# Four reorderings inside one attention round of a two-block macaron model on one Trainium2 core

## The chip, the cores and the metric

The program runs on one core of one Trainium2 chip. The metric is the device time of one execution in microseconds; lower is better. The engines are TensorE (PE in the profile; its weight loads are PEld), VectorE (DVE), ScalarE (ACT), GpSimd (POOL) and SyncE (SP, which here only issues DMAs). Each engine works through its own instruction queue in the order in which the program lists it, and the engines meet only at semaphores.

## The reference, cut to what matters

The input x has 16 sequences of 256 tokens and 128 channels, all in f32. Six residual blocks follow one another:

```
x = x + 0.5 * L0_ffn(layernorm(x))     # gated feed-forward with token shift
x = x + L0_attn(layernorm(x))          # causal attention, 16 heads of 8
x = x + 0.5 * L0_ffn(layernorm(x))     # the same feed-forward again
x = x + 0.5 * L1_ffn(layernorm(x))     # mixture of 8 experts, top 2
x = x + L1_attn(layernorm(x))          # "focus": attention iterated up to 3 times
x = x + 0.5 * L1_ffn(layernorm(x))     # the mixture again
```

The change touches the first three of them. The feed-forward (the gated one) mixes each token with the one before it, `xr = mu_r*x + (1-mu_r)*x_prev` and `xk` likewise, and gives `sigmoid(xr @ W_r) * (relu(xk @ W_k)**2 @ W_v)`. The causal attention clips its scores, takes a softmax with small epsilons in both denominators, multiplies with the values and projects the result.

## The kernel before, in words

The first three blocks run as one software pipeline over the 16 sequences, from about 55 us to 400 us of the trace. One round n (`causal_round` in each engine's program) does the attention of sequence n and, between its pieces, parts of other sequences: the normalisation and the projection behind the attention of n-1, the second feed-forward of n-2, the normalised tokens, queries, keys and values of n+2, the first feed-forward of n+3, and the statistics and normalised tokens of n+4. Rounds 0 and 1 are written out, rounds 2 to 11 are a loop of two rounds per turn, and rounds 12 to 15 are written out again. `within(n, low, high)` says which parts a written-out round has; `first` is the first feed-forward (rounds 0 to 12), `second` the second one (from round 2), `before` the back of the attention of n-1 (from round 1), `ahead` the front of n+2 (to round 13).

A round has eight steps, one for each pair of heads, hp = 0 to 7. For every pair TensorE computes the scores twice: queries in rows (`row_scores`, L1632 to L1635, into `ps_q`), of which VectorE takes the maxima (`row_maxima`, L2497, `mx`), and keys in rows (`causal_scores`, L1645 and L1646, into `ps_k`), which ScalarE exponentiates (`causal_exps`, L1173, into `e_buf`). GpSimd zeroes the part above the diagonal (L829, "keep"). For every four heads TensorE then multiplies with the values (`causal_values`, L1661 and L1658, into `ps_o`), and ScalarE copies the sums out (`evacuate_group`, L1049, `o_sb<-ps_o`).

The queues are orders written out by hand, and these waits matter for the change:

- Layer norms. VectorE takes mean and variance (`front_norm`, L2434 and L2438). ScalarE makes 1/std from them in two instructions (`token_norm`, L1054 `lnv<-mv` and L1056 `rstd<-lnv`). VectorE applies them (`front_normed`, L2443, `y<-x,mv,rstd`), and `ln_apply` waits for that `rstd`. The statistics of norm1(n+4) are applied at the very end of VectorE's round n, behind the last two maxima, `all_maxima` (L2503 to L2505) and the gating of the second feed-forward (L2466); the next instruction on VectorE is the first maximum of round n+1. The norm of n-2 behind the attention has buffers of its own (`lnv_k`, `rstd_k`, `mv_k`, `y_b`).
- Back of the attention of n-1. TensorE turns the sums over to tokens in two halves (`causal_back`, L1558, `ps_m<-ident,o_sb`) through one bank. Its second half waits for `fast_o_read`, which VectorE raises when `causal_sums(b, 0)` (L2516 and L2517) has read the first half. VectorE normalises (`causal_normalise`, L2535 to L2541, giving `o_tok`), TensorE transposes (`causal_out`, L1558, `ps_m<-ident,o_tok`), ScalarE copies (`causal_out`, L1049, `o_t`), and TensorE projects (`causal_project`, L1688).
- First feed-forward of n+3. GpSimd makes the token difference (L765), VectorE the two mixed inputs (`mix_inputs`, L2459 `xr` and L2460 `xk`, both shown as `mix<-mix,cols,y_t`), TensorE the hidden products (`ffn_hidden`, L1572 and L1574), ScalarE five activations on them (`ffn_hidden`, L1073 to L1080), GpSimd the square and gate (L769, L774), TensorE the output (L1580), ScalarE the sigmoid (L1084), VectorE the gating (L2466), and GpSimd the residual add (L779, `x<-x,mix`).
- Scores. `row_scores` of a pair waits for the maxima of the pair before it in the same bank, and `causal_scores` for the exponentials of the pair before it, since both banks are used again at once.
- `squared_lengths` (L1621) follows the last value product of the round before on TensorE, and `longest` (L2487, `qk_max`) reads it on VectorE between the maxima of pairs 0 and 1.
- `value_sums` (L1697 to L1701) ends TensorE's round; ScalarE copies it (`vs<-ps_m`).

## Time and profile before

| | |
|---|---|
| median of 3 runs | 1514.51 us (1509.53 to 1516.96) |
| the profiled execution | 1516.96 us, span 1515.2 us |
| mean granted TensorE clock | 0.962 of full speed |
| busy over the span | PE 90%, DVE 67%, ACT 57%, POOL 33% |
| causal rounds, pair 0 of round 0 to the last maximum | 55.1 to 398 us |

The span is the time from the first instruction to the last; the execution adds 1.8 us around it. The busy share of an engine is an average over stages: in the looped rounds VectorE is at 89%, not 67%. Durations are those of one profiled execution, and a duration of an instruction that overlaps the next one is longer than the distance between their starts. In a timeline row the number in square brackets is the engine's idle time in front of the instruction, with the instruction that ended it; gaps of about 0.1 us are not shown.

### The profile page before, as it was taken

Reading aid. Unit: us, or ns where it says so; the run is one execution under the profiler, and the core shown is the slowest. Engines: PE = TensorE matmul, PEld = TensorE weight load, DVE = VectorE, ACT = ScalarE, POOL = GpSimd, SP = SyncE. Lnnn points to the kernel's source line nnn. Section 1 sums busy time; section 2 is a strip of 40 time slices with the busy share of each in tenths; the row PEclk is TensorE's granted clock in tenths of the full one; section 3 lists DMA queues with packets and bytes.
Section 4 is the critical chain, followed back from the end, with each engine's and each line's share of the span. In section 5 each row is a group of like instructions: output and inputs, shape, how many; then the busy total and the mean of one; then the engine's idle time right before and its main releaser. Section 6 shows DMA issues by size and latency. Waiting matters only on the chain. (4 is left out here: it accounts for less than half of the span.)

```text
span 1515.2 us, 37569 instructions
## 1 busy us (share of the span) xinstructions
PE 1357.4 (90%) x11749; PEld 938.8 (62%) x11749; DVE 1009.2 (67%) x3281; ACT 871.2 (57%) x1595; POOL 499.1 (33%) x786
## 2 busy tenths in 40 slices
PE   4798999998689999999889998989899999899998
PEld 2566666666457777777455555555555555566876
DVE  3689889887636767677565565666666666577544
ACT  3577777776333434344567776777656667333453
POOL 5366656664210000012233233323222222004444
PEclk9799999999779999999899998999989999899999
DMA  5332233223030000001444544454534444001232
GB/s 147 76 85 64 62 83 83 57 71 83 1 86 1 12 11 11 11 11 48 120 114 125 138 121 100 124 130 111 128 93 109 112 114 102 3 8 50 83 117 77
DMA packets 75213, 116.69 MB, mean 77 GB/s; under 512 B 9401, under 2 KB 60753, under 8 KB 65876
## 3 DMA queue, kind: packets, MB, share of 16 engines
q1 hardware_dynamic: 73044, 111.05, 28.7%
q0 software_dynamic: 2048, 4.20, 0.9%
q8 instruction: 56, 0.92, 0.2%
q14 instruction: 65, 0.53, 0.1%
HBM read 85.72 MB, written 29.37 MB: 76 GB/s over the span
## 5 line engine op out<-in xcount | busy, mean ns | idle before, releaser
L1356 ACT ACTIVATE e_buf<-ps_q 128x1024 f32<-128x1024 f32 x192 | 196.5, 1023 | 106.3 <-PE ps_q L2068 106.1
L2079 PE MATMUL ps_o<-e_buf,v_st 128*32 128x256 f32 x3072 | 212.6, 396 | 4.3 <-POOL v_st L938 3.9
L1356 ACT ACTIVATE e_buf<-ps_k 128x1024 f32<-128x1024 f32 x192 | 195.6, 1019 | 19.4 <-PE ps_k L2068 17.5
L1931 PEld LDWEIGHTS ps_o<-w,e_buf 128*128 128x128 f32 x1536 | 182.8, 193 | 15.3 <-issue 13.9
L1931 PE MATMUL ps_o<-w,e_buf 128*128 128x128 f32 x1536 | 190.3, 278 | 0.0
L3023 DVE COPY o_sb<-ps_o 128x256 f32<-128x256 f32 x192 | 80.9, 422 | 113.0 <-PE ps_o L2079 68.4
L2497 DVE TENSOR_REDUCE mx<-ps_q 128x3 f32<-128x384 f32 x256 | 130.3, 548 | 27.7 <-PE ps_q L1635 27.0
L2068 PE MATMUL ps_q<-q_st,k_st 73*128 73x256 bf16 x768 | 120.6, 281 | 18.3 <-DMA q_st<-scr_q 17.6
L1173 ACT ACTIVATE e_buf<-ps_k 128x768 f32<-128x768 f32 x128 | 103.3, 807 | 48.1 <-PE ps_k L1646 46.0
L2079 PEld LDWEIGHTS ps_o<-e_buf,v_st 128*32 128x32 f32 x3072 | 81.8, 111 | 76.8 <-issue 34.5
L2068 PEld LDWEIGHTS ps_q<-q_st,k_st 73*128 73x128 bf16 x768 | 60.7, 99 | 105.5 <-issue 70.2
L1272 ACT ACTIVATE e_buf<-ps_q,b_t 128x512 f32<-128x512 f32 x96 | 65.5, 685 | 99.3 <-PE ps_q L1923 96.6
L2068 PE MATMUL ps_k<-q_st,k_st 73*128 73x256 bf16 x768 | 119.4, 279 | 3.2 <-ACT e_buf L1356 1.1
L1272 ACT ACTIVATE e_buf<-ps_k,b_t 128x512 f32<-128x512 f32 x96 | 64.8, 686 | 95.7 <-PE ps_k L1923 93.8
L829 POOL TENSOR_SCALAR_AFFINE_SELECT e_buf<-e_buf 128x512 f32<-128x512 f32 x128 | 85.7, 669 | 92.6 <-ACT e_buf L1173 91.1
L1558 PE MATMUL ps_m<-ident,o_sb 128*128 128x128 f32 x508 | 79.5, 280 | 10.5 <-DVE o_tok L2517 2.9
L1923 PE MATMUL ps_q<-mix,w 128*128 128x512 f32 x176 | 85.1, 607 | 2.5 <-issue 2.5
L2068 PEld LDWEIGHTS ps_k<-q_st,k_st 73*128 73x128 bf16 x768 | 72.9, 100 | 22.1 <-ACT e_buf L1356 13.5
L1923 PE MATMUL ps_k<-mix,w 128*128 128x512 f32 x176 | 85.1, 607 | 0.0
L912 POOL TENSOR_TENSOR rest<-qk,parts 128x512 f32<-128x512 f32 x6 | 6.9, 1156 | 235.7 <-ACT parts L1049 235.7
L1632 PE MATMUL ps_q<-mask_q,ident_b 128*128 128x256 bf16 x256 | 72.9, 285 | 9.3 <-DVEq L3311 4.5
L2774 DVE SCALAR_TENSOR_TENSOR e_buf<-ps_o,lexp,e_buf 128x128 f32<-128x128 f32 x192 | 54.0, 344 | 36.4 <-PE ps_o L1931 33.2
(397 smaller groups left out, 2913.5 us busy)
## 6 DMA issues: line engine op xcount, KB each, us to landing
q_st<-scr_q SPq DMA_DIRECT2D x64, 576.0 KB
k_st<-scr_k SPq DMA_DIRECT2D x192, 192.0 KB
scr_q<-parts SPq DMA_DIRECT2D x64, 192.0 KB, 2.1
scr_k<-parts SPq DMA_DIRECT2D x84, 64.0 KB
slots_in<-heads_out SPq DMA_DIRECT2D x2, 1536.0 KB
slots_out<-heads_out SPq DMA_DIRECT2D x12, 256.0 KB, 2.1
heads_out<-slots_in SPq DMA_DIRECT2D x10, 256.0 KB, 3.3
out_dram<-x SPq DMA_DIRECT2D x8, 256.0 KB
```

Source lines behind the costliest of these rows:

```text
L829: pool.affine_select(out=e, in_=e, compare_op=ALU.is_ge, fill=0.0, base=0, pattern=[[0, 2], [0, 2], [1, P]], channel_multiplier=-1)\
L1173: act.activation(e_buf[g % 2][:, hp * 2 % HG:hp * 2 % HG + 2, 0:3 * P], ps_k[:, :, 0:3 * P], ACT.Exp, bias=SHIFT).then_inc(sem("fast_exp"), 1)
L1272: act.activation(h_sb[e % 2][:, f, :], bank, ACT.Relu, bias=b1_t[:, j:j + 1])\
L1356: act.activation(e_buf[g % 2][:, hp * 2 % HG:hp * 2 % HG + 2, :], (ps_q, ps_k)[hp % 2][:, :, :], ACT.Exp).then_inc(sem("fast_exp"), 1)
L1558: return pe.transpose(dst, src, ident[0:k, 0:k])
L1632: mm(o[:, P:3 * P], ident_b[:, :], mask_q[:, :], start=True, stop=False, skip_group_check=True)
L1923: mm(bank, w1[:, e, f * P:(f + 1) * P], mixed(m, u)[:, :], start=True, stop=True)\
L1931: last = mm(ps_o[:, e % 2, t * P:(t + 1) * P], h_sb[e % 2][:, f, t * P:(t + 1) * P], w2[:, e * NF + f, :], start=f == 0, stop=f == NF - 1)
L2068: last = mm(bank[:, u, t * T:(t + 1) * T], k_st[p][0:ROWS_P1, hp * 2 + u, t * P:(t + 1) * P], q_st[p][0:ROWS_P1, hp * 2 + u, :], start=Tru ...
L2079: last = mm(ps_o[VW * j:VW * j + VW, g % 2, 0:T], v_st[p][:, kt, HG * g + j, :], e_buf[g % 2][:, j, kt * T:(kt + 1) * T], start=kt == 0, s ...
L2497: red(mx[:, h, :], ps_q[:, u, 0:3 * P].rearrange("p (c k) -> p c k", c=3), AX.X, ALU.max)\
L3023: dve.tensor_copy(o_sb[:, g, :], ps_o[:, g % 2, 0:T]).then_inc(sem("fast_evac"), 1)
```

## The change

Four places of the round change their order; nothing is added or taken away.

```diff
--- before.py
+++ after.py
@@ -1215,9 +1215,9 @@
                 causal_exps(n, 4)
                 if isinstance(n, int) and n == B - 2:
                     mix_norm(0)
-                evacuate_group(n, 1)
                 if before:
                     causal_out(n - 1)
+                evacuate_group(n, 1)
                 causal_exps(n, 5)
                 if ahead:
                     normed_tokens(n + 2)
@@ -1233,12 +1233,12 @@
                 evacuate_group(n, 2)
                 if second:
                     ffn_sigmoid(mix2(n - 2))
-                if within(n, 0, B - 5):
-                    token_norm(norm1(n + 4), mv, lnv, rstd)
                 causal_exps(n, 7)
                 if ahead:
                     causal_values(n + 2)
                 value_sums(n)
+                if within(n, 0, B - 5):
+                    token_norm(norm1(n + 4), mv, lnv, rstd)
                 if before:
                     token_norm(norm3(n - 1), mv_k, lnv_k, rstd_k)
 
@@ -1735,9 +1735,9 @@
                         if first:
                             ffn_out(mix1(n + 3), 0)
                     elif hp == 4:
-                        causal_values(n, p, 1)
                         if before:
                             causal_out(b)
+                        causal_values(n, p, 1)
                     elif hp == 5:
                         if before:
                             causal_project(b)
@@ -2586,10 +2586,10 @@
                 if within(n, B - 2, B - 2) and isinstance(n, int):
                     dve.wait_ge(sem("F_x"), mix2(GB - 1) + 1 + 1)
                     mix_stats(0, 0)
+                if first:
+                    mix_inputs(mix1(n + 3))
                 if before:
                     causal_sums(b, 0)
-                if first:
-                    mix_inputs(mix1(n + 3))
                 row_maxima(n, 2)
                 if before:
                     causal_sums(b, 1)
```

1. ScalarE copies the transposed attention output of n-1 (`causal_out`) ahead of the second group of sums (`evacuate_group(n, 1)`).
2. ScalarE makes 1/std for norm1(n+4) (`token_norm`) behind the last exponentials, the copy of the values and the copy of the value sums, where it stood ahead of all three.
3. TensorE transposes the attention output of n-1 ahead of the second value product.
4. VectorE makes the mixed inputs of the first feed-forward ahead of the first half of the attention sums.

ScalarE's queue at the end of the second round (n = 1), the difference of the two programs; `lnv` and `rstd` are the norm that is moved, `v_tok` and `vs` the two copies, `lnv_k` and `rstd_k` the norm behind the attention:

```order
 L1159 ACTIVATE squares<-qk 128x512
 L1049 ACTIVATE o_sb<-ps_o 128x256
-L1054 ACTIVATE lnv<-mv 128x2
-L1056 ACTIVATE rstd<-lnv 128x2
 L1173 ACTIVATE e_buf<-ps_k 128x2x384
 L1049 ACTIVATE v_tok<-ps_m 128x256
 L1049 ACTIVATE vs<-ps_m 128x384
+L1054 ACTIVATE lnv<-mv 128x2
+L1056 ACTIVATE rstd<-lnv 128x2
 L1054 ACTIVATE lnv_k<-mv_k 128x2
 L1056 ACTIVATE rstd_k<-lnv_k 128x2
```

The two instructions of the norm pass the exponentials of pair 7 and both copies, and now stand directly ahead of the other norm. SyncE's and GpSimd's queues stay as they are.

VectorE's queue in an early round, from `longest` to the sums; `mix<-mix,cols,y_t` are xr and xk, `s_sum` and `o_tok` the first half of the attention sums:

```order
 L2487 TENSOR_REDUCE qk_max<-ps_o 16x2
 L2497 TENSOR_REDUCE mx<-ps_q 128x3 x2
+L2459 SCALAR_TENSOR_TENSOR mix<-mix,cols,y_t 128x256
+L2460 SCALAR_TENSOR_TENSOR mix<-mix,cols,y_t 128x256
 L2516 TENSOR_SCALAR s_sum<-ps_m,low_behind 128x16
 L2517 SCALAR_TENSOR_TENSOR o_tok<-vs,ps_m 128x128
-L2459 SCALAR_TENSOR_TENSOR mix<-mix,cols,y_t 128x256
-L2460 SCALAR_TENSOR_TENSOR mix<-mix,cols,y_t 128x256
 L2497 TENSOR_REDUCE mx<-ps_q 128x3 x2
 L2516 TENSOR_SCALAR s_sum<-ps_m,low_behind 128x16
```

Four instructions change places in pairs: the mixed inputs now come first, and the read of the first half, which frees the bank, second.

TensorE's queue at pair 4 of an early round; `ps_o<-e_buf,v_st` is the second value product, `ps_m<-ident,o_tok` the transposes of the attention output:

```order
 L1645 MATMUL ps_k<-q_st,k_st 128x128
 L1646 MATMUL ps_k<-q_st,k_st 128x256
-L1661 MATMUL ps_o<-e_buf,v_st 32x256 x4
-L1658 MATMUL ps_o<-e_buf,v_st 32x128 x4
 L1558 MATMUL ps_m<-ident,o_tok 128x128 x2
+L1661 MATMUL ps_o<-e_buf,v_st 32x256 x4
+L1658 MATMUL ps_o<-e_buf,v_st 32x128 x4
 L1632 MATMUL ps_q<-mask_q,ident_b 128x256
 L1633 MATMUL ps_q<-k_st,q_st 128x256
```

The two transposes pass the eight small products of the value group.

## Rows read from the trace of the kernel before

**Rows 1.** Windows: ten looped rounds, then a stretch of the last rounds.
```profile
core 0: us, PE busy (x) PEld busy (x) DVE busy (x) ACT busy (x) POOL busy (x), PEclk, DMA share, GB/s
93.90:311.80 217.90, 198.78 (x2032) 149.04 (x2030) 193.22 (x561) 162.74 (x410) 139.21 (x199) 1.00 0.29 73
...
364.70:371.50 6.80, 6.19 (x32) 5.15 (x33) 4.21 (x11) 2.45 (x6) 1.25 (x2) 0.50 0.54 122
```

**Rows 2.** Timeline of VectorE around one looped round (the eighth), from its start.
```profile
start us, us, engine line op out<-in xcount [idle before <-releaser]
...
202.28 0.59 DVE L2443 TENSOR_SCALAR y<-x,mv,rstd 128x128 f32 x2
202.80 1.01 DVE L2497 TENSOR_REDUCE mx<-ps_q 128x3 f32<-128x384 f32 x2
203.88 0.92 DVE L2443 TENSOR_SCALAR y<-x,mv_k,rstd_k 128x128 f32 x2
205.18 0.68 DVE L2487 TENSOR_REDUCE qk_max<-ps_o 16x512 f32 x1 [0.38 <-PE ps_o L1621]
205.79 1.00 DVE L2497 TENSOR_REDUCE mx<-ps_q 128x3 f32<-128x384 f32 x2
...
207.14 0.79 DVE L2459 SCALAR_TENSOR_TENSOR mix<-mix,cols,y_t 128x256 f32<-128x256 f32 x1
207.85 0.85 DVE L2460 SCALAR_TENSOR_TENSOR mix<-mix,cols,y_t 128x256 f32<-128x256 f32 x1
...
215.96 0.47 DVE L2460 SCALAR_TENSOR_TENSOR mix<-mix,cols,y_t 128x256 f32<-128x256 f32 x1
...
216.69 0.59 DVE L2443 TENSOR_SCALAR y<-x,mv,rstd 128x128 f32 x2
...
222.16 1.02 DVE L2497 TENSOR_REDUCE mx<-ps_q 128x3 f32<-128x384 f32 x2 [1.04 <-PE ps_q L1635]
...
224.13 0.59 DVE L2443 TENSOR_SCALAR y<-x,mv,rstd 128x128 f32 x2
```

**Rows 3.** Timeline of ScalarE, same round: its start and its last third.
```profile
201.74 0.19 ACT L1054 ACTIVATE lnv<-mv 128x2 f32<-128x2 f32 x1
201.97 0.20 ACT L1056 ACTIVATE rstd<-lnv 128x2 f32<-128x2 f32 x1
202.08 0.79 ACT L1173 ACTIVATE e_buf<-ps_k 128x768 f32<-128x768 f32 x1
...
203.03 0.49 ACT L1049 ACTIVATE vs<-ps_m 128x384 f32<-128x384 f32 x1
203.40 0.21 ACT L1054 ACTIVATE lnv_k<-mv_k 128x2 f32<-128x2 f32 x1
...
218.69 0.38 ACT L1073 ACTIVATE mix<-ps_o 128x256 f32<-128x256 f32 x1 [0.50 <-PE ps_o L1574]
...
223.81 0.20 ACT L1056 ACTIVATE rstd<-lnv 128x2 f32<-128x2 f32 x1
```

**Rows 4.** Timeline of GpSimd, same round: the residual add.
```profile
203.73 0.73 POOL L779 TENSOR_TENSOR x<-x,mix 128x256 f32 x1
```

**Rows 5.** Timeline of TensorE, same round.
```profile
206.48 0.27 PE L1632 MATMUL ps_q<-mask_q,ident_b 128*128 128x256 bf16 x1
...
207.46 0.60 PE L1558 MATMUL ps_m<-ident,o_sb 128*128 128x128 f32 x4
208.76 0.71 PE L1572 MATMUL ps_m<-w_t,mix 128*128 128x128 f32 x4 [0.69 <-DVE mix L2460]
...
213.81 0.64 PE L1661 MATMUL ps_o<-e_buf,v_st 128*32 128x256 f32 x8
...
214.77 0.44 PE L1558 MATMUL ps_m<-ident,o_tok 128*128 128x128 f32 x2
215.24 0.28 PE L1632 MATMUL ps_q<-mask_q,ident_b 128*128 128x256 bf16 x1
...
217.33 0.44 PE L1558 MATMUL ps_m<-ident,y 128*128 128x128 f32 x2 [0.41 <-DVE y L2443]
```

**Rows 6.** Waits in the ten looped rounds: VectorE on the squared lengths.
```profile
DVE qk_max L2487 <- PE ps_o L1621: 3.5, 9, 0.4
```

**Rows 7.** Timeline of VectorE at the start of the second round.
```profile
74.32 1.02 DVE L2497 TENSOR_REDUCE mx<-ps_q 128x3 f32<-128x384 f32 x2 [0.39 <-issue]
```

**Rows 8.** Timeline of TensorE in the fifteenth round.
```profile
365.31 0.40 PE L1632 MATMUL ps_q<-mask_q,ident_b 128*128 128x256 bf16 x1 [1.47 <-DVE mx L2497]
```

## The prediction

> **What bounds the kernel now.** I read the windows by stage first, since all four edits lie in the causal rounds. The ten looped rounds take 217.9 us, 21.79 us each, with VectorE busy for 193.22 us (89%) and TensorE for 198.78 us (91%) at a granted clock of 1.00 [rows 1]. The reader is to see that no engine is full, but two are near it, so a round is a ring through several queues. Its length is found by following one thing round, and I follow the normalised tokens `y` of norm1(n+4), the last instruction of VectorE's round.
>
> They start at 202.28, and again at 224.13, 21.85 us later [rows 2]. From 202.28 VectorE works through its queue to the other `y` (norm2), which ends at 216.69 + 0.59 = 217.28. In these 15.00 us the one idle time worth naming is 0.38 us before `longest`, ended by the squared lengths on TensorE [rows 2]. TensorE has waited 0.41 us for that `y` and starts on it at 217.33 [rows 5]; ScalarE gets the products at 218.69 after 0.50 us of idle time, and from there to the `rstd` of norm1 at 223.81 its queue has eleven rows and no wait for another engine [rows 3]. That `rstd` ends at 224.01, and `y` starts 0.12 us later [rows 2, 3]. One round earlier it is the same: end 201.97 + 0.20 = 202.17, `y` at 202.28. So the ring is 15.00 us of VectorE and 6.85 us of TensorE and ScalarE, and `rstd` stands on it with no slack. The 1.04 us that VectorE idles before the maxima of pair 7 at 222.16 [rows 2] is a wait inside the second part and not spare time behind it.
>
> **The norm on ScalarE (edit 2).** It removes nothing and moves two instructions behind three. Now the exponentials of pair 7 start at 202.08, `lnv` at 201.74. After the edit the exponentials take the place of `lnv` (201.74, 0.34 us earlier), `vs` follows 203.03 - 202.08 = 0.95 us behind them at 202.69, the next instruction 203.40 - 203.03 = 0.37 us later at 203.06, and `rstd` 0.23 us after that, ending at 203.49 [rows 3]. That is 1.32 us later than 202.17. VectorE's `y` would start at 203.60 instead of 202.28. Behind it on VectorE stand the maxima of pair 0, for which TensorE waits before pair 1, and everything else of the round. The norm of n-2 keeps its time (its `lnv_k` now starts at 203.40 as before, since the same work is ahead of it).
>
> Of the 1.32 us the idle time before `longest` gives 0.38 us back, as VectorE then arrives after the squared lengths; it is up to 0.4 us and 3.5 us in nine of the loop's rounds [rows 6]. Nothing else in the 15.00 us is idle, so the maxima of pair 1 come at 205.79 + 0.94 = 206.73. The second part of the ring grows by the whole 1.32 us. The ring is longer by 0.94 us. This holds for the ten looped rounds: 9.4 us. Rounds 0 and 1 have the same end of round, but the first maximum behind round 0 idles 0.39 us anyway [rows 7], and both lose the wait at `longest`: 1.32 - 0.39 - 0.38, about 0.6 us, twice, 1.2 us. Rounds 12 to 15 have no norm1. Sum: 10.6 us.
>
> **What collides.** The times of VectorE depend on GpSimd beside it. The `y` of norm n-2 took 0.92 us, the other `y` of the same shape 0.59 [rows 2], while GpSimd's residual add ran from 203.73 to 204.46 [rows 4]. After the edit the add comes 0.34 us earlier (it follows the last "keep", which follows the exponentials), to 203.39 to 204.12, and it then lies under the moved `y` at 203.60. I take the 0.33 us as moved from one `y` to the other, cost 0. The ends are a gain of 0.33 us a round, if nothing collides, and a loss of 0.5 us; over 12 rounds -4 to +6 us.
> The Trainium skill ("SBUF — State Buffer", section "Who interferes with whom") says that VectorE in a two-port mode and GpSimd take a shared port pair by an exclusive lock, and that the second to issue blocks fully. The row bears it out: the tail of the slowed `y` is 204.80 = 204.46 + 0.34. By that rule the moved `y` would stand until 204.12, 0.52 us, where the old one lost 0.33, and the sum would be about 2 us higher.
>
> **The mixed inputs on VectorE (edit 4).** Now the first half of the sums is read from 206.79 (205.79 + 1.00), the mixed inputs run 207.14 to 208.70, and TensorE, 0.69 us idle, starts the hidden products at 208.76 [rows 2, 5]. The inputs would come 0.35 us earlier. But TensorE's second half of the transposes stands ahead of the hidden products, and it needs the bank that the first half's read frees. It starts at 207.46 without a wait now; after the edit it can start only when inputs and read are both done, at 208.70 plus the shift of the round, and the hidden products 0.44 us behind it. So the edit gains nothing and makes the hidden products about 0.4 us later. I cost it at nothing for the ring; what hides it is VectorE's own work between the read of the sums and the maxima of pair 3 (the second half of the sums, the denominators, the statistics of norm2). If that cover were gone it would cost 0.4 us in each of 13 rounds, 5 us.
>
> **The transposes on TensorE and the copy on ScalarE (edits 3 and 1).** The transposes start at 214.77, as soon as `o_tok` is there, so the value group now fills the time ahead of them [rows 5]. It goes from 213.81 to about 214.6. After the edit it runs behind them: transposes to 215.05 (0.28 us), value group to 215.85, and so the scores of pair 5 start 0.6 us later than 215.24, where the second of them waited for VectorE's maxima anyway. The 0.41 us of idle time at 217.33 and that wait cover it, barely [rows 5]. Cost 0, ends -0.1 (the projection comes sooner) and +0.3 us a round.
>
> **The clock.** With both halves late, TensorE would wait twice within a short stretch: before pair 2, which it starts at 206.48 now and which then needs the first of the two maxima from 206.73, there at 207.23, 0.75 us; and before the second transposes, where it arrives about 0.8 us later than the 207.46 of now and VectorE is done at 208.70 + 0.94 = 209.64, 1.4 us. Nothing like it stands in the looped rounds of before, whose clock never left 1.00 [rows 1]. In the fifteenth round TensorE waited 1.47 us in one piece [rows 8], and the 6.8 us from 364.7 on ran at 0.50, that is at 1.2 GHz instead of 2.4 [rows 1]. Two microseconds of waiting so close together may do the same. The 6.8 us at half the clock cost TensorE at most 3.4 us of work. Its waits and VectorE's own chain cover much of that, so I take five such falls in the ten rounds at 0.8 us each, a quarter of it: 4 us. The ends are none (0) and one in each round at half of it, 1.7 us (17).
>
> **The sum.** 10.6 + 0 + 0 + 0 + 4 = 14.6 us. Against the profiled execution (1516.96 us: span 1515.2 and 1.8 around it) that gives 1531.6. It was the slowest of the three; its median is 2.45 us lower, and against the median I forecast 1529.
>
> **The rivals.**
> - Faster. The exponentials and the "keep" of pair 7 come 0.34 us earlier, so the last value group and the squared lengths come earlier, and the 0.38 us before `longest` vanish without a price. That decides if `rstd` has 0.94 us or more of slack before `y`; then 12 rounds give 12 x 0.38 = 4.6 us, and with half a microsecond a round from the earlier inputs up to 10: 1505 to 1510. For it: the wait at `longest` is real [rows 6]. Against it: 0.12 us between `rstd` and `y`, in both rounds shown. Chance 0.05.
> - The shift is swallowed. The collisions with GpSimd dissolve (0.33 us in `y`, and something of the 0.79 and 0.85 us of the mixed inputs, where the same two instructions take 0.47 for the second feed-forward [rows 2]), as VectorE slips against it; with 0.6 us of that gained it is 0.94 - 0.6 = 0.34 us a round and no clock falls: 4 us, 1518.5. For it: GpSimd's chain hangs on ScalarE and does not slip along at first. Against it: its cast and third split simply follow under the same two instructions. Chance 0.11.
> - The edits stay beside the path, because the ring is elsewhere: 1514.5. Against it stands that the ring closes to 0.1 us. Chance 0.03.
> - The clock falls in every looped round: 10.6 + 17 = 28 us, 1542. For it: two waits of 2.1 us in sum. Against it: rounds and clock need not keep step. Chance 0.06.
> - My forecast, 8 to 24 us slower: 0.75.
>
> **How the numbers follow.** A difference within 0.5% (7.6 us) is about what measurement can't tell from none. Slower by more: 0.75 + 0.06 and a little of the second rival, 0.82. The same: 0.13. Faster: 0.05. The range takes 10.6 us with the collisions' gain (-4) at the lower end, 1521, widened to 1520 for the second rival, and at the upper end 10.6 + 4 + 6 + half of what more the clock may take, 1541.
>
> **What would show it.** In the profile after, `rstd` of norm1 stands between `vs` and `lnv_k`, and VectorE idles about 1.2 us before the last `y` of rounds 0 to 11. The idle time at `longest` is gone. TensorE idles over 1 us before the second `ps_m<-ident,o_sb` group, and its 0.69 us before L1572 are gone. A looped round lasts 22.7 us, or 23.5 with a fall of the clock, and stretches at 0.50 appear between 94 and 320 us. A looped round at or below 21.8 us, or a `y` that starts as early against the maxima of pair 7 as now, would prove the main step wrong; a clock of 1.00 throughout, the last term.

## The result, and the profile after

| | before | after |
|---|---|---|
| median of 4 runs | 1512.28 us (1509.53 to 1516.96) | 1533.62 us (1530.47 to 1540.83) |
| the profiled execution | 1516.96 us, span 1515.2 | 1536.57 us, span 1534.8 |
| mean granted TensorE clock | 0.962 | 0.955 |

The ratio is 1.0156, with a 95% interval of 1.0126 to 1.0187: slower by 21.3 us by the medians and by 19.6 us by the two profiled executions. The forecast was 14.6 us slower than the profiled execution, 1529 us at the median, with a range of 1520 to 1541. The direction held and the result lies in the range; the size was too small, by 5.0 us of 19.6.

The windows show where it went. The columns are those of [rows 1], the first row is the ten looped rounds again, and the second is one of the short stretches in which the clock fell.

```profile
core 0: us, PE busy (x) PEld busy (x) DVE busy (x) ACT busy (x) POOL busy (x), PEclk, DMA share, GB/s
92.30:329.40 237.10, 203.85 (x2032) 153.93 (x2031) 196.31 (x560) 160.98 (x410) 140.07 (x199) 0.96 0.26 67
...
194.50:197.90 3.40, 3.40 (x18) 2.50 (x22) 2.52 (x11) 0.54 (x2) 1.30 (x3) 0.50 0.27 77
```

The rounds take 237.1 us instead of 217.9. That is 19.2 of the 19.6 us. Rounds 12 to 15 add 4.0 us, the stretch ahead of the loop is 0.4 us shorter, and everything behind round 15 is 3.2 us shorter. VectorE does only 3 us more work than in [rows 1] and TensorE 5 us more, so most of the new time is waiting. The clock is at 0.96 over the stretch, where it was at 1.00: it fell six times, at 122.8, 146.7, 194.5, 218.4, 266.1 and 290.0. The last row is the third of these falls, at 0.50, the lower level of 1.2 GHz; each of the six lasted 3.4 us. I take a round from one `top<-mx` (L2504, once a round) to the next. The ten were 21.25 to 22.38 us long before and 21.79 on average. Now the four without a fall last 22.48 to 23.04 us (the first 22.48, the others 22.85 to 23.04) and the six with one 24.15 to 24.41.

The loop has two rounds per turn, and its steady rounds (those without a fall, from n = 4 on) alternate between two kinds: before, 21.84 us for odd n and 21.74 for even n. The kinds differ inside as well: [rows 2] is an odd round (n = 7, the eighth), where `y<-x,mv_k,rstd_k` takes 0.92 us, and in the even rounds it takes 0.70.

This is VectorE in the seventh round of after (n = 6, a looped round, with a fall in it), from its start, answering [rows 2]. The idle time before an instruction and what ended it stand in brackets, as there.

```profile
188.34 0.82 DVE L2443 TENSOR_SCALAR y<-x,mv,rstd 128x128 f32 x2 [1.19 <-ACT rstd L1056]
189.08 1.02 DVE L2497 TENSOR_REDUCE mx<-ps_q 128x3 f32<-128x384 f32 x2
190.02 1.24 DVE L2443 TENSOR_SCALAR y<-x,mv_k,rstd_k 128x128 f32 x2
191.18 0.67 DVE L2487 TENSOR_REDUCE qk_max<-ps_o 16x512 f32 x1
191.78 1.00 DVE L2497 TENSOR_REDUCE mx<-ps_q 128x3 f32<-128x384 f32 x2
192.71 0.63 DVE L2459 SCALAR_TENSOR_TENSOR mix<-mix,cols,y_t 128x256 f32<-128x256 f32 x1
193.27 0.84 DVE L2460 SCALAR_TENSOR_TENSOR mix<-mix,cols,y_t 128x256 f32<-128x256 f32 x1
...
195.77 0.23 DVE L2516 TENSOR_SCALAR s_sum<-ps_m,low_behind 128x16 f32<-128x16 f32 x1 [0.39 <-PE ps_m L1558]
...
198.93 1.02 DVE L2497 TENSOR_REDUCE mx<-ps_q 128x3 f32<-128x384 f32 x2 [1.02 <-PE ps_q L1635]
```

The reader is to see four things. `y` now waits 1.19 us for `rstd`. The idle time before `qk_max` is gone. The two `y` and the mixed inputs have durations other than before (this is an even round: before, its two `y` take 0.59 and 0.70 us). And behind the fall at 194.5 there are two new waits for TensorE, 0.39 and 1.02 us.

ScalarE at the same place, answering [rows 3]: the norm behind the copies, as the order said.

```profile
186.53 0.80 ACT L1173 ACTIVATE e_buf<-ps_k 128x768 f32<-128x768 f32 x1
187.22 0.38 ACT L1049 ACTIVATE v_tok<-ps_m 128x256 f32<-128x256 f32 x1
187.48 0.50 ACT L1049 ACTIVATE vs<-ps_m 128x384 f32<-128x384 f32 x1
187.85 0.22 ACT L1054 ACTIVATE lnv<-mv 128x2 f32<-128x2 f32 x1
188.10 0.20 ACT L1056 ACTIVATE rstd<-lnv 128x2 f32<-128x2 f32 x1
```

TensorE in the same round, answering [rows 5]. The first row's wait stands before pair 2, the second's before the second half of the transposes, the third's before those of the attention output. L1572 has no wait any more.

```profile
192.38 0.28 PE L1632 MATMUL ps_q<-mask_q,ident_b 128*128 128x256 bf16 x1 [1.00 <-DVE mx L2497]
...
194.50 1.11 PE L1558 MATMUL ps_m<-ident,o_sb 128*128 128x128 f32 x4 [0.89 <-DVE o_tok L2517]
195.41 1.06 PE L1572 MATMUL ps_m<-w_t,mix 128*128 128x128 f32 x4
...
202.12 0.44 PE L1558 MATMUL ps_m<-ident,o_tok 128*128 128x128 f32 x2 [1.18 <-DVE o_tok L2541]
```

The first hidden products (L1572) take 1.06 us instead of 0.71 [rows 5], at half the clock.

### The profile page after: what moved, and what is told of

The parts are those of the page before. It is cut to its first block and busy times, and to the rows that moved or that the text cites. A ratio compares the mean times of both kernels' runs of the same rounds, so it can differ in the third digit from the quotient of the medians.

```text
span 1534.8 us, 37569 instructions
## 1 busy us (share of the span) xinstructions
PE 1361.5 (89%) x11749; PEld 946.6 (62%) x11749; DVE 1013.5 (66%) x3281; ACT 869.0 (57%) x1595; POOL 499.0 (33%) x786
## 5 line engine op out<-in xcount | busy, mean ns | idle before, releaser
L829 POOL TENSOR_SCALAR_AFFINE_SELECT e_buf<-e_buf 128x512 f32<-128x512 f32 x128 | 84.1, 657 | 96.4 <-ACT e_buf L1173 93.7
L1558 PE MATMUL ps_m<-ident,o_sb 128*128 128x128 f32 x508 | 83.2, 289 | 20.9 <-DVE o_tok L2517 13.3
L1558 PEld LDWEIGHTS ps_m<-ident,o_sb 128*128 128x128 f32 x508 | 60.0, 146 | 33.2 <-DVE o_tok L2517 16.7
```

The source lines that it names most:

```text
L829: pool.affine_select(out=e, in_=e, compare_op=ALU.is_ge, fill=0.0, base=0, pattern=[[0, 2], [0, 2], [1, P]], channel_multiplier=-1)\
L1558: return pe.transpose(dst, src, ident[0:k, 0:k])
```

## The experiments

norm_only, inputs_only, out_only and all_but_norm were timed beside runs of the kernel before that took 1570 us; beside the others it took 1514. No trace of the kernel before is kept from there. The trace of out_only shows steady rounds of 21.72 and 21.82 us, as long as those of before, and the 55 us behind the causal rounds; their cause was not examined. So only ratios to the runs of before beside them, and the lengths of the looped rounds, are compared. The expectations were written when the result of after was known; the 20 or 21 us that they name are its loss.

**norm_only: edit 2 alone.**

```diff
-                if within(n, 0, B - 5):
-                    token_norm(norm1(n + 4), mv, lnv, rstd)
                 causal_exps(n, 7)
...
                 value_sums(n)
+                if within(n, 0, B - 5):
+                    token_norm(norm1(n + 4), mv, lnv, rstd)
```

> Edit 2 alone (1/std of norm1(n+4) behind the copies on ScalarE). Ring theory: a looped round is 22.8 to 23.2 us instead of 21.8, VectorE idle about 1.2 us before the last y, which over 12 rounds is 12 to 14 us; TensorE's waits before pair 2 and before the hidden products come to 1.6 us a round and are less close together, so at most three falls of the clock at 1.3 us: 12 to 18 us slower in all. Rival (the swap on VectorE and TensorE's second wait carry most of it): under 7 us slower.

Ratio 1.0033 (1.0018 to 1.0047). The looped rounds took 223.1 us, +5.2, of which about 1.5 is one fall of the clock. The steady rounds lasted 22.07 (odd) and 22.27 (even), where before they lasted 21.84 and 21.74: +0.24 and +0.52, +0.38 us on average. The time is that of the rival (under 7 us), but its reason is not: the wait that the ring theory named is there. VectorE in an odd round:

```profile
251.69 0.91 DVE L2443 TENSOR_SCALAR y<-x,mv,rstd 128x128 f32 x2 [1.19 <-ACT rstd L1056]
...
253.45 0.95 DVE L2443 TENSOR_SCALAR y<-x,mv_k,rstd_k 128x128 f32 x2
...
256.19 0.47 DVE L2459 SCALAR_TENSOR_TENSOR mix<-mix,cols,y_t 128x256 f32<-128x256 f32 x1
256.59 0.47 DVE L2460 SCALAR_TENSOR_TENSOR mix<-mix,cols,y_t 128x256 f32<-128x256 f32 x1
256.98 1.00 DVE L2497 TENSOR_REDUCE mx<-ps_q 128x3 f32<-128x384 f32 x2
```

The wait for `rstd` is there in full, but the round is not 0.94 us longer. The two rows of `y` together are 0.35 us longer than in [rows 2]. Still, from `y` to the maxima of pair 2 it is 256.98 - 251.69 = 5.29 us, where before it was 6.35 (202.28 to 208.63). The wait at `longest` gives 0.38 of that. The mixed inputs give 0.70, since they take 0.47 us each instead of 0.79 and 0.85 [rows 2]. GpSimd in the same stretch, first in before and then in norm_only:

```profile
206.49 1.16 POOL L806 TENSOR_TENSOR rest<-qk,parts 128x512 f32<-128x512 f32 x1
207.81 0.61 POOL L810 CAST parts<-rest 128x512 bf16<-128x512 f32 x1 [0.17 <-POOL rest L806]
208.38 0.82 POOL L829 TENSOR_SCALAR_AFFINE_SELECT e_buf<-e_buf 128x512 f32<-128x512 f32 x1
```

```profile
254.28 1.16 POOL L806 TENSOR_TENSOR rest<-qk,parts 128x512 f32<-128x512 f32 x1
255.61 0.61 POOL L810 CAST parts<-rest 128x512 bf16<-128x512 f32 x1 [0.17 <-POOL rest L806]
256.18 1.38 POOL L829 TENSOR_SCALAR_AFFINE_SELECT e_buf<-e_buf 128x512 f32<-128x512 f32 x1
```

`rest` and the cast split the queries and keys into parts. Before, the two mixed inputs start under `rest` and under the cast, and end 0.28 us behind each (207.93 and 208.70, against 207.65 and 208.42). In norm_only they start at 256.19, when the cast ends (256.22), and it is GpSimd's `keep` (L829) that is longer, 1.38 us for 0.82 before. Its row starts 0.01 us ahead of the mixed input's, so the rows do not say which of the two came first. The late norm moved VectorE out of a collision in which it used to wait.

**inputs_only: edit 4 alone.**

```diff
+                if first:
+                    mix_inputs(mix1(n + 3))
                 if before:
                     causal_sums(b, 0)
-                if first:
-                    mix_inputs(mix1(n + 3))
```

> Edit 4 alone (mixed inputs ahead of the first half of the sums on VectorE). Ring theory: rstd is on time, the ring keeps its 21.8 us; the hidden products come 0.4 us later on TensorE, covered; 0 to 3 us slower, the clock stays at full speed in the looped rounds. Rival (the swap carries it): 8 us slower or more, with falls of the clock between 94 and 320 us.

Ratio 1.0075 (1.0059 to 1.0091), 12.9 us by the medians: the rival came true, and the cost that the prediction put at nothing is there. The looped rounds took 229.9 us, +12.0. Rounds without a fall lasted 22.48 and 22.59 us: +0.75. In four rounds the clock fell, and these lasted 23.7 to 23.8. VectorE in an even round:

```profile
282.32 1.00 DVE L2497 TENSOR_REDUCE mx<-ps_q 128x3 f32<-128x384 f32 x2
283.25 1.16 DVE L2459 SCALAR_TENSOR_TENSOR mix<-mix,cols,y_t 128x256 f32<-128x256 f32 x1
284.34 0.85 DVE L2460 SCALAR_TENSOR_TENSOR mix<-mix,cols,y_t 128x256 f32<-128x256 f32 x1
...
286.93 0.52 DVE L2524 SCALAR_TENSOR_TENSOR s_u<-emax,s_sum 128x32 f32<-128x32 f32 x1
...
287.69 0.61 DVE L2528 SCALAR_TENSOR_TENSOR s_den<-s_u,s_sum 128x32 f32<-128x32 f32 x1
```

GpSimd:

```profile
282.98 1.15 POOL L806 TENSOR_TENSOR rest<-qk,parts 128x512 f32<-128x512 f32 x1
284.30 0.61 POOL L810 CAST parts<-rest 128x512 bf16<-128x512 f32 x1 [0.17 <-POOL rest L806]
...
285.66 1.16 POOL L814 TENSOR_TENSOR parts<-rest,parts 128x512 bf16<-128x512 f32 x1
286.77 0.64 POOL L829 TENSOR_SCALAR_AFFINE_SELECT e_buf<-e_buf 128x512 f32<-128x512 f32 x1
287.62 0.63 POOL L769 TENSOR_TENSOR mix<-mix 128x256 f32<-128x256 f32 x1 [0.22 <-ACT mix L1073]
```

The first mixed input stands from 283.25 to 284.41, and GpSimd's `rest` ends at 284.13; the second stands until 285.19, and the cast ends at 284.91. Each ends 0.28 us after the GpSimd instruction beside it. The read of the sums in this place, two instructions 0.35 us long together, had let the first part of `rest` pass; now it comes on top. From the maxima of pair 1 to those of pair 2 it is 3.13 us (282.32 to 285.45), where it was 2.80 in the even rounds of before (2.84 in the odd one of [rows 2]): +0.33. From there to the maxima of pair 3 it is 3.63, where before it was 3.20: +0.43, since `s_u` and `s_den` take 0.52 and 0.61 us beside GpSimd's `keep` and square; a short instruction between them, `s_du`, gives 0.25 us of that back. Before:

```profile
210.09 0.29 DVE L2524 SCALAR_TENSOR_TENSOR s_u<-emax,s_sum 128x32 f32<-128x32 f32 x1
...
210.87 0.18 DVE L2528 SCALAR_TENSOR_TENSOR s_den<-s_u,s_sum 128x32 f32<-128x32 f32 x1
```

VectorE waits for nothing between these maxima, and the two stretches make up the whole 0.75 us. TensorE meanwhile waits 1.5 us in one piece for the read of the bank, in each of the ten rounds (14.4 us in all), and in four of them the clock fell.

**inputs_small_split and before_small_split: edit 4, and the kernel before, with GpSimd's first two split operations made smaller.** In the looped rounds `rest` and its cast work on 8 of 256 columns, so these kernels leave out most of the lower parts of the queries and keys.

```diff
-                pool.tensor_tensor(rest[:, :, :], qk32[:, :, :], parts[:, :, 0, :], ALU.subtract)\
+                c = slice(0, T) if isinstance(f, int) else slice(0, 8)
+                pool.tensor_tensor(rest[:, :, c], qk32[:, :, c], parts[:, :, 0, c], ALU.subtract)\
...
-                pool.tensor_copy(parts[:, :, 1, :], rest[:, :, :]).then_inc(sem("part_mid"), 1)
+                pool.tensor_copy(parts[:, :, 1, c], rest[:, :, c]).then_inc(sem("part_mid"), 1)
```

> Edit 4 alone, and in the looped rounds GpSimd's first two split operations (the f32 remainder and its bf16 copy, each 128 x 512) work on 8 columns instead of 256 for each of queries and keys, so the lower parts of the split are stale. Port theory (the swap costs 0.7 us a round only because the mixed inputs then queue behind GpSimd's split for the shared port): the mixed inputs run in 0.5 to 0.65 us each, a looped round without a fall of the clock is 21.0 to 21.5 us, no slower than its twin without edit 4. Rival (TensorE's wait for the freed bank is what lengthens the round): 0.5 us or more a round slower than the twin.

> The twin: the kernel before with the same two small split operations in the looped rounds, so the lower parts of the split are stale. Port theory: the mixed inputs fall from 0.79 and 0.85 us to 0.5 to 0.65, a looped round from 21.8 to 21.0 to 21.4 us, the kernel 4 to 8 us faster than before. Rival (VectorE's durations are its own): 21.8 us a round.

With the smaller split, edit 4 costs nothing: 21.42 and 21.47 us a round, 0.11 to 0.15 less than the 21.53 and 21.62 of its twin. The ratios to the kernel before with the whole split are 0.9996 (0.9972 to 1.0020) and 0.9990 (0.9967 to 1.0014). So the port theory's forecast for the pair came true. Of the twin alone it was too high: rounds of 21.0 to 21.4 us and a kernel 4 to 8 us faster did not come. VectorE with edit 4, and then without:

```profile
225.57 1.00 DVE L2498 TENSOR_REDUCE mx<-ps_q 128x3 f32<-128x384 f32 x2
226.50 0.46 DVE L2460 SCALAR_TENSOR_TENSOR mix<-mix,cols,y_t 128x256 f32<-128x256 f32 x1
226.89 0.47 DVE L2461 SCALAR_TENSOR_TENSOR mix<-mix,cols,y_t 128x256 f32<-128x256 f32 x1
```

```profile
226.96 0.48 DVE L2460 SCALAR_TENSOR_TENSOR mix<-mix,cols,y_t 128x256 f32<-128x256 f32 x1
227.36 0.86 DVE L2461 SCALAR_TENSOR_TENSOR mix<-mix,cols,y_t 128x256 f32<-128x256 f32 x1
```

The order is that of inputs_only; only the neighbours on GpSimd are short (`rest` 0.22 us, the cast 0.41). From the maxima of pair 1 to those of pair 2 it is now 2.05 us (225.57 to 227.62), against 2.49 in the twin. The next stretch keeps its loss (3.63 against 3.31, with `s_u` 0.52 and `s_den` 0.61 as in inputs_only). So edit 4's +0.33 became -0.44, and the sign of the whole edit turned on what GpSimd ran beside it. TensorE's wait for the bank fell from 1.5 to 0.3 us with it, since the read comes sooner, so this pair takes the collision and the wait away together. That the wait is not what costs is seen in inputs_only: its steady rounds have no idle time on VectorE between the maxima of pairs 1 and 3, and that stretch holds the whole loss. The smaller split saves the kernel before 2.1 us in the loop, no more, since its second mixed input then stands beside a `keep`.

**out_only: edits 1 and 3 alone.**

```diff
-                evacuate_group(n, 1)
                 if before:
                     causal_out(n - 1)
+                evacuate_group(n, 1)
...
-                        causal_values(n, p, 1)
                         if before:
                             causal_out(b)
+                        causal_values(n, p, 1)
```

> Edits 1 and 3 alone (attention output transposed ahead of the second value group, and its copy ahead of theirs). Ring theory: covered by the 0.4 us that TensorE waits for the norm2 y, within 2 us of before on either side. Rival (TensorE arrives late at y each round): 0.3 us in each of 15 rounds, 4 to 5 us slower.

Ratio 1.0008 (0.9989 to 1.0028). Steady rounds lasted 21.72 and 21.82, as before, so the ring doesn't feel these edits. Two rounds with a fall, which the kernel before has not, lasted 23.83 and 23.29, and the ten rounds 221.2 us, +3.3, in the profiled execution. TensorE waits for `o_tok`, where the value group used to fill the time (first row), and after the fall VectorE waits for the projection (second row).

```profile
216.54 0.44 PE L1558 MATMUL ps_m<-ident,o_tok 128*128 128x128 f32 x2 [1.07 <-DVE o_tok L2541]
```

```profile
220.89 0.42 DVE L2547 TENSOR_TENSOR x<-x,ps_m 128x256 f32 x1 [0.90 <-PE ps_m L1688]
```

**all_but_norm (edits 1, 3, 4) and all_but_inputs (edits 1, 2, 3): the whole without one part.** Each is after with one of the two diffs above taken back.

> Edits 1, 3 and 4 together, without the norm. Ring theory: between 0 and 4 us slower than before, looped rounds of 21.8 to 22.1 us and no fall of the clock in them; so the norm is worth 17 us or more of the 21. Rival: most of the loss stays, 10 us slower or more.

> Edits 1, 2 and 3 without the swap on VectorE. Port theory (the late norm shifts VectorE so that its mixed inputs come ahead of GpSimd's zeroing and run undisturbed at 0.47 us each; the swap puts them back under GpSimd's split): like the norm alone, looped rounds of 22.0 to 22.3 us, the mixed inputs at 0.47 us, at most two falls of the clock, 4 to 8 us slower. Rival (parts add up without interaction: whole minus swap, 20 - 12): 8 us or more, with the mixed inputs at 0.8 us.

Without the norm 1.0077 (1.0051 to 1.0103), rounds of 22.5 us and with a fall 23.8 to 24.0, of which there were five: the rival came true. Without the mixed inputs 1.0032 (1.0002 to 1.0061), rounds of 22.05 and 22.25, two with a fall, and the mixed inputs at 0.47 us: the port theory came true. Edit 4 is the dearest part. In the steady rounds the parts add up in size: +0.38 and +0.75 are 1.13 us a round, and after has 22.86 and 23.04, +1.16.

They do not add up in place. Between after and norm_only, edit 4 costs 0.78 us a steady round, but of another make than in inputs_only. From the maxima of pair 1 to those of pair 2 it is 2.60 us for 2.05, since the mixed inputs, at 0.63 and 0.84 us, now lie beside the cast and a `keep`. To the maxima of pair 3 it is 0.1 us less. From there to those of pair 4 it is 3.17 for 2.80, where the two `corr` instructions (L2535 and L2539) take about 0.6 and 0.67 us beside GpSimd's gate and a `keep`, for 0.42 and 0.48. `s_u` and `s_den` keep their short times. That 0.75 and 0.78 are so near is luck.

**after_again and after_filled: the whole once more, and with TensorE kept busy in its two waits.** The fillers are products into a bank that nobody reads at that time.

```diff
+            def filler(count):
+                for _ in range(count):
+                    mm(ps_m[:, 0, 0:P], ident_b[:, :], mask_q[:, 0:P], start=True, stop=True)
...
+                    if hp == 2 and before and first:
+                        pe.wait_ge(sem("T_ytc"), norm1(n + 3) + 1)
+                        filler(10)
...
                             causal_back(b, 0)
...
+                        if before and first:
+                            filler(16)
                             causal_back(b, 1)
```

> The changed kernel itself, on the chip of the four parts. Both theories: looped rounds of 22.8 to 23.2 us, 24.1 to 24.5 us where the clock falls, 18 to 22 us slower than before in all. It is here so that parts and whole are measured against the same runs of before.

> The changed kernel with 26 small bf16 matmuls a round of which no result is used (10 ahead of the row scores of pair 2, 16 ahead of the second half of the transposes), so that TensorE works where it waited. Clock theory: no fall between 94 and 340 us, all looped rounds 22.8 to 23.2 us, 8 to 11 us faster than the changed kernel, so 9 to 12 us slower than before. Rival (the falls cost nothing, the waits would be there anyway): same time as the changed kernel or slower by the added work, with the rounds at 24 us staying.

after_again was timed beside runs of the kernel before at 1514.59 us, not beside those of the four first parts. It took 1537.78 us, ratio 1.0172 (1.0122 to 1.0223); after_filled beside the same runs 1522.78, ratio 1.0063 (1.0038 to 1.0088). No fall is left in the looped rounds; all but the first last 22.86 to 23.10 us. The windows of the looped rounds of after_filled:

```profile
93.00:322.00 229.00, 209.72 (x2289) 162.93 (x2289) 195.95 (x558) 160.52 (x409) 140.31 (x199) 1.00 0.27 69
```

and TensorE in it, the same two places as in after:

```profile
188.94 0.72 PE L1705 MATMUL ps_m<-mask_q,ident_b 128*128 128x128 bf16 x10
190.11 0.28 PE L1632 MATMUL ps_q<-mask_q,ident_b 128*128 128x256 bf16 x1 [0.44 <-DVE mx L2506]
...
191.19 1.06 PE L1705 MATMUL ps_m<-mask_q,ident_b 128*128 128x128 bf16 x16
192.25 0.66 PE L1558 MATMUL ps_m<-ident,o_sb 128*128 128x128 f32 x4
```

The wait of 1.00 is down to 0.44 and that of 0.89 is gone, while what TensorE waited for comes no sooner: from `y` to the maxima of pair 2 VectorE takes the same 6.0 us in both. The third wait, 1.3 us before the transposes of the attention output, is left in it. The loop is 229.3 us long against 235.8 in after_again, which had five falls in it: 1.3 us each. By the end of round 15 the two are 8.0 us apart, of 16.9 us between the two profiled executions (15.0 between the medians). The rest lies behind the causal rounds, where the two kernels are the same. There the trace of after_filled has 66.0 us at a clock of 0.50 and that of after_again 76.9, but after has 86.3 in a stretch no longer than after_again's, so the clock alone does not explain it, and the cause stays open.

**early_scores and late_sums: two orders meant to beat before.** The first lets ScalarE finish the norm ahead of the splits, and TensorE give pair 7's scores ahead of the second output; the second moves the value sums behind the next round's first scores and the last value product behind the squared lengths, and lets ScalarE make both norms and the query and key copies ahead of the exponentials of pair 7. Their core, of early_scores first:

```diff
-                if ahead:
-                    causal_parts(n + 2)
-                evacuate_group(n, 2)
                 if second:
                     ffn_sigmoid(mix2(n - 2))
                 if within(n, 0, B - 5):
                     token_norm(norm1(n + 4), mv, lnv, rstd)
+                if ahead:
+                    causal_parts(n + 2)
+                evacuate_group(n, 2)
...
+                    elif hp == 7:
                         if second:
                             ffn_out(mix2(n - 2), 1)
                         causal_values(n, p, 2)
-                    elif hp == 7:
```

On TensorE in late_sums, at the first pair of the next round:

```diff
-                        if before:
-                            causal_values(b, 1 - p, NGV - 1)
                         if within(n, 1, B - 2):
+                            value_sums(b, 1 - p)
                             squared_lengths(n + 1)
+                        if before:
+                            causal_values(b, 1 - p, NGV - 1)
```

> The kernel before with two other moves: ScalarE makes the sigmoid of the second feed-forward and 1/std of norm1(n+4) directly behind the exponentials of pair 6 (ahead of the queries' and keys' parts), and TensorE does the output product of the second feed-forward and the third value group behind the scores of pair 7. Ring theory: the 1.04 us that VectorE idles before pair 7 goes and rstd is there 2 us sooner, so a looped round is 20.8 to 21.3 us and the kernel 6 to 11 us faster than before. Rival (VectorE or the other queues take it back, in port waits or at the last exponentials): within 3 us of before.

> A candidate on the kernel before, for rounds 0 to 13: ScalarE makes the sigmoid and both norms right behind the exponentials of pair 6 and those of pair 7 ahead of the high parts; TensorE takes the third value group behind the scores of pair 7 and the value sums behind the scores of the next round's pair 0, where it now waits for the zeroing. The last try left VectorE waiting 1.5 us for the scores of pair 0, which stood behind 7.7 us of TensorE's own work. Ring theory: that work shrinks by 1.1 us, a looped round is 20.8 to 21.2 us, the kernel 7 to 11 us faster than before. Rival (another queue closes the ring at 21.8 us): within 2 us of before.

early_scores: 1.0041 (1.0015 to 1.0066), steady rounds 21.99 and 22.08. late_sums: 1.0014 (0.9995 to 1.0033), steady rounds 21.79 and 21.84, those of before. In both the rival came true: the ring closes again elsewhere. VectorE in early_scores:

```profile
226.61 1.02 DVE L2497 TENSOR_REDUCE mx<-ps_q 128x3 f32<-128x384 f32 x2 [1.65 <-PE ps_q L1635]
```

and in late_sums:

```profile
226.00 1.02 DVE L2526 TENSOR_REDUCE mx<-ps_q 128x3 f32<-128x384 f32 x2 [0.72 <-PE ps_q L1658]
228.16 0.68 DVE L2516 TENSOR_REDUCE qk_max<-ps_o 16x512 f32 x1 [0.62 <-PE ps_o L1644]
```

With `rstd` early, VectorE waits for TensorE's scores of pair 0 instead, and in late_sums for the squared lengths too. That TensorE's own round is about as long as the norm's ring is what I read from this; it was not tested by itself. None of these kernels is faster than before clear of noise.

## Why the prediction was right, and where its size was off

The loop grew by 19.2 us. Its parts, the edits each run alone and the clock from after:

| | forecast, loop | measured |
|---|---|---|
| edit 2, the norm | 0.94 a round, 9.4 | 0.38 a round, 3.7 (norm_only, less its one fall) |
| edit 4, the mixed inputs | 0 | 0.75 a round, 7.1 (inputs_only, less its four falls) |
| edits 1 and 3 | 0 | 0 but for falls |
| the clock | five falls at 0.8, 4 | six falls at 1.4, 8.4 (after) |
| sum | 13.4 | 19.2 |

- **The mechanism of the norm held.** `rstd` stands on the ring without slack. VectorE waits 1.19 us for it in every looped round whose wait the profile lists (10.7 us in nine), and 1.44 at the end of round 0; 1.32 later was forecast. From `top<-mx` to `y` a steady round of norm_only takes 1.28 us more. Around the first two rounds nothing is settled: from the mark of round 0 to that of round 1 it is 0.63 us more in after, where about 0.6 was forecast, but it is also 0.63 with edit 4 alone and 0.76 with the norm alone.
- **The step "The ring is longer by 0.94 us" was mis-sized**: 0.38. Of the 1.28 us, the stretch from `y` to the maxima of pair 1 gave back 0.14 on average (0.26 in odd rounds, 0.02 in even ones) and not 0.38, and the stretch of the mixed inputs gave back 0.76 and not 0. The step held the durations of the mixed inputs fixed. Moved against GpSimd, they fell from 0.79 and 0.85 us to 0.47 each. The second rival had named just this ("0.94 - 0.6 = 0.34 us a round") and was right on its own part; I gave it 0.11 because I believed that GpSimd's cast and split simply follow under the same instructions. They don't: in norm_only `rest` starts 2.59 us behind `y` and before 4.21, so GpSimd did not slip along.
- **The collision of the moved `y`** came too, 0.59 to 0.91 us in the odd rounds, 0.32 against the 0.33 that I had moved from one `y` to the other. But the other `y` kept its time, 0.92 and now 0.95. In the even rounds, which the prediction did not look at, the two went from 0.59 and 0.70 to 0.82 and 1.23. So the cost 0 was wrong, by 0.35 and 0.76 us of longer instructions. They took the place of the idle time at `longest`, which is gone, and that is why so little of the 0.38 came back.
- **The step that costed edit 4 at nothing failed.** I looked at TensorE's bank wait and held it covered, and in the steady rounds of inputs_only it is: VectorE does not idle behind it, though it is 1.5 us long. (In three of the four rounds with a fall VectorE then waits 0.2 to 0.4 us for the second transposes.) What I did not price was what lay beside the instructions in their new place. Alone, the mixed inputs started right under `rest`, which runs 1.15 us; in after they lay beside the cast and a `keep`. The sentence "the inputs would come 0.35 us earlier" was false. My bound for the edit, 0.4 us a round, was drawn from the bank wait alone and did not hold 0.75.
- The Trainium skill ("SBUF — State Buffer", section "Who interferes with whom") says that the port pair which VectorE and GpSimd share is an exclusive lock, and that a VectorE instruction with two inputs in SBUF contends with a GpSimd instruction that reads SBUF. The rows of inputs_only agree: both mixed inputs end 0.28 us after the GpSimd instruction beside them. I used the lock in the prediction for one `y` only. Used for the mixed inputs it would have said from the rows of before that they end no sooner than now, with the 0.35 us of the read behind them; measured is +0.33. The other 0.43 of the 0.75, `s_u` and `s_den`, I would not have found by it, since their place against GpSimd depends on all that comes ahead.
- **Edits 1 and 3** cost the ring nothing, as forecast. They take the cover from a wait of TensorE (1.07 us before the transposes in out_only, 1.18 in after), and where the clock falls there, a round is 1.5 to 2 us longer.
- **The clock** fell six times where five were forecast, behind waits of 1.00 and 0.89 us where 0.75 and 1.4 were forecast. Its price was too small: 1.4 us a round, not 0.8. I had taken a quarter of what a fall of 6.8 us costs TensorE at most. These falls lasted 3.4 us each, which costs it at most 1.7 us of work (an estimate, half of 3.4), and most of that came through. VectorE's chain did not cover it, as the new waits of 0.39 and 1.02 us behind the fall show. That the same two waits stand in all ten rounds (8.4 and 8.9 us in the waits of the loop) and only six have a fall agrees with the fourth rival's "rounds and clock need not keep step". after_filled shows that the falls of after hang on these two waits: it keeps the third and longest one, before the transposes of the attention output (13.1 us in ten rounds), and has no fall.
- **The signs** came: the idle time before `y`, none at `longest`, none before L1572, stretches at 0.50, rounds of 22.9 (22.7 forecast) and 24.3 (23.5 forecast). The wait before the second transposes is 0.89 us and not over 1.

So that the total fell into the range is luck in part: the errors had both signs, -5.7 for the norm, +7.1 for edit 4, +4.4 for the clock. The direction did not hang on luck, since the norm, edit 4 and the clock each made the loop longer by itself.

## What to carry to other kernels

Before pricing a move on VectorE, lay GpSimd's timeline beside the new place and the old: the same instruction took 0.47 or 1.16 us in two orders of one kernel. In a loop of two rounds per turn do so for both rounds. A wait that reads as a full microsecond can be worth a third of it when the shift also undoes a collision, and an edit that makes VectorE wait for nothing new can be the dearest. Where a change makes TensorE wait twice close together, as here 1.00 and 0.89 us, price the work behind a fall of the clock at half speed without assuming that other waits cover it.

## What the runs showed of the hardware

- `SCALAR_TENSOR_TENSOR` 128x256 in f32 took 0.46 to 0.48 us at its shortest (both mixed inputs in norm_only and inputs_small_split), and 1.16 where it started 0.27 us behind the start of a 1.15 us subtraction on GpSimd (inputs_only). Beside the cast, a `keep` or the end of the subtraction it took 0.63 to 0.85 (before, after, inputs_only). In the longer cases of before, inputs_only and after it ended 0.27 or 0.28 us behind the GpSimd instruction. Two of 128x32, 0.18 or 0.19 us at their shortest (after), took 0.52 and 0.61 (inputs_only).
- The blocking goes both ways. GpSimd's `keep` took 0.82 us in before, and 1.38 in norm_only, where VectorE's mixed inputs started with it.
- 26 small bf16 products in TensorE's waits (1.78 us of it by their rows) kept its clock at 1.00 through ten rounds (after_filled), where it fell six and five times without them (after, after_again). By themselves they cost nothing that shows: rounds of 22.86 to 23.10 with them, 22.85 to 23.04 in those of after without a fall.
- With one wait of 1.5 us in every round (inputs_only) the clock fell in four rounds of ten, and with the pair of 1.00 and 0.89 us in six (after) or five (after_again). With one wait of 0.69 us before the hidden products in each round (before) it fell in none.
